# Sharing each loaded weight tile between two token halves in the expert stage of an eight-core recurrent-block and mixture-of-experts kernel

## What is computed

```
logits = xt @ gate_w.T;  scores = softmax(logits);  two experts are chosen per token -> cw[t, e]
h1 = einsum('td,efd->etf', xt, w1) + b1        # 8 experts, f = 2048, even and odd f are two halves
h3 = einsum('td,efd->etf', xt, w3) + b3
a  = swiglu(h1 * h3)                            # g = min(h[::2], 7), l = clip(h[1::2], -7, 7)
                                                # g * sigmoid(1.702 g) * (l + 1)
y  = einsum('etf,edf->etd', a, w2) + b2
out = sum_e cw[t, e] * y[e] + shared expert     # the shared expert has the same form
```

## Time and profile before

| | us |
|---|---|
| median of 7 runs | 5578.23 (5573.30 to 6060.81) |
| profiled execution, its own time | 5568.08 |
| its span on the slowest core (core 6) | 5566.5 |
| spans of the 8 cores | 5528.0 to 5566.5 |
| granted TensorE clock, mean, every core | 0.892 to 0.895 |
| TensorE matmul busy | 4030.7 (72%), 16176 recorded |
| TensorE weight load busy | 1617.7 (29%), 16496 |
| VectorE busy | 2357.5 (42%) |
| ScalarE busy | 1289.6 (23%) |
| POOL busy | 633.0 (11%) |

### The profile page before, as it was taken

One profiled execution on the slowest core, in us unless ns is written; L12 is line 12 of the kernel. 1 busy time (PEld: TensorE's weight loads), 2 busy tenths in 40 slices (PEclk: granted clock), 3 DMA queues, 4 the chain that ended last, 5 costly groups with the idle time before them and its releaser, 6 DMA issues.

```text
span 5566.5 us, 52221 instructions; the slowest of 8 cores (5528.0 to 5566.5 us)
## 1 busy us (share of the span) xinstructions
PE 4030.7 (72%) x16176; PEld 1617.7 (29%) x16496; DVE 2357.5 (42%) x3808; ACT 1289.6 (23%) x1875; POOL 633.0 (11%) x1187
## 2 busy tenths in 40 slices
PE   4565565664555666688889888887588888888885
PEld 1122121221211221233333333331233333333331
DVE  2433433323324233444554444544544554444544
ACT  1332332413224141111121111121111221111221
POOL 1011010111100111011111111110011111111110
PEclk8788788787887977899999999998799999999997
DMA  5354353435433442233334333332133343333341
GB/s 72 51 86 65 49 83 56 78 42 79 59 57 53 60 77 34 38 61 61 64 56 76 56 68 61 65 55 55 28 59 66 54 74 63 61 65 65 55 73 40
DMA packets 179709, 336.68 MB, mean 60 GB/s; under 512 B 19456, under 2 KB 39952, under 8 KB 179312
## 3 DMA queue, kind: packets, MB, share of 16 engines
q0 software_dynamic: 175280, 324.92, 36.1%
q1 hardware_dynamic: 4160, 8.39, 0.4%
HBM read 649.41 MB, written 8.39 MB: 118 GB/s over the span
## 4 chain that ended last, share of the span: by engine, by line
PE 64%; DVE 12%; ACT 11%; DMA 7%; issue 5%; DVEq 0%; POOL 0%; ACTq 0%; another core or an unknown queue 0%; POOLq 0%
PE pb L165 63%; ACT bufA L908 4%; DMA wi<-wi_xh 3%; DMA wi<-wi_gate 2%; DVE sa L532 1%; DVE sa L517 1%; ACT L513 1%; ACT ssf L513 1%; ACT sa L584 1%; DMA wo<-wout 1%; ACT L566 1%; DMA wg<-wgates 1%; DVE ssi L529 1%; DVE ssi L526 1%; ACT ssi L566 1%
## 5 line engine op out<-in xcount | busy, mean ns | idle before, releaser
L165 PE MATMUL pb<-xn,wq 128*128 128x512 bf16 x9030 | 2028.3, 379 | 275.8 <-ACT bufA L908 265.6
L165 PEld LDWEIGHTS pb<-xn,wq 128*128 128x128 bf16 x9216 | 882.1, 98 | 1427.8 <-issue 409.6
L165 PE MATMUL pb<-sxh,wg 128*128 128x512 bf16 x2256 | 592.5, 423 | 383.7 <-ACT ssf L566 361.2
L165 PE MATMUL pb<-a_s,w2s 128*128 128x512 bf16 x2258 | 544.5, 401 | 126.8 <-DVE a_s L963 124.5
L908 ACT ACTIVATE bufA<-pb,c_b1g 128x512 f32<-128x512 f32 x256 | 175.9, 687 | 1675.0 <-PE pb L165 1675.0
L165 PE MATMUL pb<-sxnbf,wi 128*128 128x512 bf16 x1128 | 315.1, 423 | 293.4 <-DMA wi<-wi_gate 127.5
L913 DVE SCALAR_TENSOR_TENSOR bufA<-pb,c_b3g,bufA 128x512 f32<-128x512 f32 x256 | 192.2, 751 | 672.7 <-ACT bufA L908 672.7
L165 PEld LDWEIGHTS pb<-sxh,wg 128*128 128x128 bf16 x2304 | 237.9, 106 | 738.0 <-issue 540.1
L165 PEld LDWEIGHTS pb<-a_s,w2s 128*128 128x128 bf16 x2304 | 231.7, 102 | 431.6 <-issue 195.0
L942 DVE TENSOR_TENSOR bufA<-bufA,bufC 128x512 f32<-128x512 f32 x288 | 199.5, 693 | 241.0 <-ACT bufC L937 241.0
L937 ACT ACTIVATE bufC<-bufA 128x512 f32<-128x512 f32 x288 | 181.3, 629 | 467.4 <-DVE bufA L932 467.4
(11 more groups left out here) (148 smaller groups left out, 3022.1 us busy)
## 6 DMA issues: line engine op xcount, KB each, us to landing
wg<-wgates POOLq DMA_DIRECT2D x192, 384.0 KB, 5.0
wq<-w1g POOLq DMA_DIRECT2D x128, 256.0 KB, 3.8
wq<-w3g POOLq DMA_DIRECT2D x128, 256.0 KB, 4.6
wq<-w1l POOLq DMA_DIRECT2D x128, 256.0 KB, 6.1
wq<-w3l POOLq DMA_DIRECT2D x128, 256.0 KB, 6.9
w2s<-w POOLq DMA_DIRECT2D x128, 256.0 KB, 4.1
wi<-wi_xh POOLq DMA_DIRECT2D x96, 256.0 KB, 3.9
wi<-wi_gate POOLq DMA_DIRECT2D x48, 256.0 KB, 4.5
```

What stands on the lines that cost most here:

```text
L165: t.matmul(o, l, r, start=s1, stop=s2),
```

## The change

The two token halves of a weight slice are run one behind the other, and the second of the two matmuls loads no weights.

- The four quadrants are split in two: a "G half" (quadrants 0 and 1) and an "L half" (2 and 3), 32 matmuls each. In each, k is the outer loop, and for each k four matmuls follow each other: first quadrant half 0, first quadrant half 1, second quadrant half 0, second quadrant half 1, into banks 0, 1, 2, 3. Both halves use the banks 0 to 3.
- After the G half come t1 of both halves on ScalarE, gg and g7 of both on VectorE, then sg and p1. After the L half come t2 of both, and ll, lc, p2, as of half 0 and then of half 1.
- Weight slots of quadrants 0 and 1 are released after the G half, those of 2 and 3 after the L half.
- In w2, k is the outer loop too: banks 4 and 5 in turn, 16 matmuls, then both `racc` additions.
- A new function after the build, `_mark_ldweights_reuse`, goes through TensorE's list and sets `ldweights=False` on each bf16 matmul whose weights are those of the matmul before it. This marks 4608 of the 9216 matmuls of the quadrants, 1152 of the 2304 of w2, 16 of the 32 b2 matmuls, and 120 of the 128 one-column matmuls of the first norm in the recurrent part.

The order of the other stages is the same. The diff, cut to its core:

```diff
+                            for k in range(NC_D):
+                                for j, (q_, t) in enumerate(
+                                        ((0, 0), (0, 1), (1, 0), (1, 1))):
+                                    b = 2 * q_ + t
+                                    t_mm(pb[b][:, :], wq[q_].slot(ql[q_])[:, k, :],
+                                         xn2[:, k, slice(t * ST, (t + 1) * ST)],
+                                         start=(k == 0), stop=(k == NC_D - 1),
+                                         waits=((bank_wait(b) if k == 0 else [])
...
+                            wq[0].done(ql[0])
+                            wq[1].done(ql[1])
+                            tcG = S.n["t"]
...
+                                a_op(lambda a, t=t, b_=bias(c_b1g, c_sb1g): a.activation(
+                                        out=bufA[:, t, :], in_=pb[t][:, :],
+                                        func=AF.Identity, bias=b_, scale=1.0),
+                                     waits=[("t", tcG)]
...
+                            bank_guard[0] = ("a", a1[0])
+                            bank_guard[1] = ("a", a1[1])
+                            bank_guard[2] = ("v", gg_v[0])
+                            bank_guard[3] = ("v", gg_v[1])
...
+                            for k in range(NC_D):
+                                for j, (q_, t) in enumerate(
+                                        ((2, 0), (2, 1), (3, 0), (3, 1))):
+                                    b = 2 * (q_ - 2) + t
...
+                            bank_guard[0] = ("a", a2[0])
+                            bank_guard[1] = ("a", a2[1])
+                            bank_guard[2] = ("v", ll_v[0])
+                            bank_guard[3] = ("v", ll_v[1])
...
-                                for k in range(E):
-                                    t_mm(pb[b][:, :], w2s.slot(li)[:, k, :],
-                                         a_s[:, k, tloc],
...
+                            for k in range(E):
+                                for t in range(2):
+                                    b = 4 + t
+                                    t_mm(pb[b][:, :], w2s.slot(li)[:, k, :],
+                                         a_s[:, k, slice(t * ST, (t + 1) * ST)],
...
+def _mark_ldweights_reuse(nc):
...
+                    key = (w.memref, w.offset, str(w.ap), str(w.dtype))
+                    both_bf16 = (w.dtype == mybir.dt.bfloat16
+                                 and ins.ins[0].dtype == mybir.dt.bfloat16)
+                    if key == last and both_bf16:
+                        new = dataclasses.replace(
+                            ins, name=nc.get_next_instruction_name(),
+                            ldweights=False)
```

More of the change, by code:

```diff
@@ new lines, in build_nc @@
+                            for t in range(2):
+                                v_op(lambda v, t=t, b_=bias(c_b3g, c_sb3g): v.scalar_tensor_tensor(
+                                        out=bufA[:, t, :], in0=pb[2 + t][:, :],
+                                        scalar=b_, in1=bufA[:, t, :],
+                                        op0=OP.add, op1=OP.mult),
+                                     waits=[("t", tcG), ("a", a1[t])],
+                                     tag=f"gg{p}{e}{m}{t}")
+                                gg_v[t] = S.n["v"]
+                                v_op(lambda v, t=t: v.tensor_scalar(
+                                        out=bufA[:, t, :], in0=bufA[:, t, :],
+                                        scalar1=7.0, scalar2=None, op0=OP.min),
+                                     tag=f"g7{p}{e}{m}{t}")
+                                g7_v[t] = S.n["v"]
@@ new lines, in build_nc @@
+                            for t in range(2):
+                                v_op(lambda v, t=t: v.tensor_tensor(
+                                        out=bufA[:, t, :], in0=bufA[:, t, :],
+                                        in1=bufC[:, t, :], op=OP.mult),
+                                     waits=[("a", sg_a[t])], tag=f"p1{p}{e}{m}{t}")
+                            for k in range(NC_D):
+                                for j, (q_, t) in enumerate(
+                                        ((2, 0), (2, 1), (3, 0), (3, 1))):
+                                    b = 2 * (q_ - 2) + t
+                                    t_mm(pb[b][:, :], wq[q_].slot(ql[q_])[:, k, :],
+                                         xn2[:, k, slice(t * ST, (t + 1) * ST)],
+                                         start=(k == 0), stop=(k == NC_D - 1),
+                                         waits=((bank_wait(b) if k == 0 else [])
+                                                + ([wq[q_].wait(ql[q_])]
+                                                   if (k == 0 and t == 0) else [])),
+                                         tag=f"ql{q_}{p}{e}{m}{t}")
@@ new lines, in build_nc @@
+                            wq[2].done(ql[2])
+                            wq[3].done(ql[3])
+                            tcL = S.n["t"]
+                            a2 = {}
+                            ll_v = {}
+                            for t in range(2):
+                                a_op(lambda a, t=t, b_=bias(c_b1l, c_sb1l): a.activation(
+                                        out=bufB[:, t, :], in_=pb[t][:, :],
+                                        func=AF.Identity, bias=b_, scale=1.0),
+                                     waits=[("t", tcL)], tag=f"t2{p}{e}{m}{t}")
+                                a2[t] = S.n["a"]
@@ L892, in build_nc @@
                             for t in range(2):
                                 tloc = slice(t * ST, (t + 1) * ST)
[L894 to L911, removed]
@@ L922, in build_nc @@
[L922 to L928, removed]
@@ L946, in build_nc @@
[L946 to L947 removed]
+                                v_op(lambda v, t=t, b_=bias(c_b3l, c_sb3l): v.scalar_tensor_tensor(
+                                        out=bufB[:, t, :], in0=pb[2 + t][:, :],
+                                        scalar=b_, in1=bufB[:, t, :],
+                                        op0=OP.add, op1=OP.mult),
+                                     waits=[("a", a2[t])], tag=f"ll{p}{e}{m}{t}")
@@ L961, in build_nc @@
                                          tag=f"p2{p}{e}{m}{t}")
[L962 to L968, removed]
+                                v_op(lambda v, t=t, m=m, tloc=tloc: v.tensor_tensor(
+                                        out=a_s[:, m, tloc], in0=bufA[:, t, :],
+                                        in1=bufB[:, t, :], op=OP.mult),
+                                     tag=f"as{p}{e}{m}{t}")
+                                as_prev[t] = ("v", S.n["v"])
+                            bank_guard[0] = ("a", a2[0])
+                            bank_guard[1] = ("a", a2[1])
+                            bank_guard[2] = ("v", ll_v[0])
+                            bank_guard[3] = ("v", ll_v[1])
                         as_done = ("v", S.n["v"])
@@ L977, in build_nc @@
                                 b = 4 + t
-                                for k in range(E):
-                                    t_mm(pb[b][:, :], w2s.slot(li)[:, k, :],
-                                         a_s[:, k, tloc],
[L981 to L991, removed]
+                                tc = stop_tc[t]
                                 if e == 0:
@@ L1085, in _ @@
                 S.replay("gpsimd", gpsimd, sems)
+    _mark_ldweights_reuse(nc)
     return nc
+def _mark_ldweights_reuse(nc):
+    import dataclasses
+    for f in nc.m.functions:
+        for bl in f.blocks:
+            il = bl.instructions
+            last = None
+            for i, ins in enumerate(il):
+                if isinstance(ins, mybir.InstMatmult):
+                    if ins.is_transpose:
+                        last = None
+                        continue
+                    w = ins.ins[1]
+                    key = (w.memref, w.offset, str(w.ap), str(w.dtype))
[5 more added lines that the diff above has]
+                            ldweights=False)
+                        il[i] = new
+                        nc.register_instruction(new)
+                    last = key
+                elif isinstance(ins, mybir.InstEventSemaphore):
+                    continue
+                else:
+                    last = None
 def _prep_shared(i):
```

80 lines of the change are left out of this document (49 added, 31 removed).

## The result

The changed kernel takes 6809.48 us (median of 12 runs, 6785.67 to 7080.03) and is 1.2219 times the kernel before (95% interval 1.2181 to 1.2257): some 1230 us slower than the median of before. The forecast was 6790.

A forecast was written before the change was run, and what follows sets the result against it. The expert stage was taken as bound by matmul column flow plus 0.98 us per handover. Losses of 220 + 392 + 181 + 418 = 1211 us on the profiled 5568 gave 6779, plus 10 for the median, rounded to 6790; range 6360 to 7010.

The forecast's parts named there:

- G to L handover: From G half to L half, bank 3's matmul waits for the second gg: 1.53 us lost, 144 times, 220 us.
- L to G handover: From L half to next G half, bank 3's matmul waits for the second ll: 3.11 us lost, 126 times, 392 us.
- w2: Between w2 output tiles, the next tile's second matmul waits for the second addition: 1.44 us lost, 126 times, 181 us.
- clock after G to L: TensorE's clock falls after the G to L stall: half of 1.69 us, 0.85, lost 144 times, 122 us.
- clock after L to G: TensorE's clock falls after the L to G stall: 2.35 us lost, 126 times, 296 us.
- weight loads: 5760 loads dropped from the two big loops lie under the matmuls: at most 14 us back, taken as nothing.
- signs named beforehand: Profile after: some 144 gg and 126 ll waits (over 2 us each), `racc` waits, some 5900 fewer loads, unchanged spacing, lower clock.
- Rival 1: In the m loop the stalls are as computed but the clock holds at 1.00: 6371 us, chance 0.14.
- Rival 2: The clock falls at every handover of the m loop: 7005 us, chance 0.12.
- Rival 3: Handovers are shorter because VectorE or ScalarE give the banks up sooner: about 6185 us, chance 0.05.
- Rival 4: Two matmuls with kept weights overlap, so the kernel is not slower: 5545 us, chance 0.03.
- note that p1 and the loads stay hidden: p1 fits under the L half and POOL's loads keep their order: costed at nothing.

The follow-up runs named there:

- e10: The changed kernel unaltered, run once more and profiled at 6781.68 us; 1.2189 times the kernel before.
- e4: The changed kernel with w2 in the old order (8 matmuls into bank 4, then 8 into bank 5); shortest 6602.01 us.
- e3: The changed kernel plus 1836 matmuls with unread results, put into idle bank 4 during the handover stalls; shortest 6375.08 us.
- e1: The changed kernel without the marks, so every matmul loads its weights again; 1.2229 times the kernel before, shortest 6797.67 us.
- e6: The kernel before with kept weights shared one quadrant at a time, 16 matmuls into two banks while two are read; 0.941 of the kernel before.
- e7: The kernel of e6 with every matmul loading its weights again; 0.9425 of the kernel before, shortest 5252.47 us.
- e5: The kernel before, same matmul order, but each bank read after its own 8 matmuls instead of all 32; shortest 5175.41 us.

## Why the prediction was right

Its terms, and what the runs and the trace of e10 gave. For the handovers I took the starts of all 9216 quadrant matmuls of that trace: the mean time from a half's last start to the fourth start of the next, less 0.38 for the last one's row and 1.63 for the same place before; for the clock, the time from the fourth to the 32nd start less 28 x 0.216. Before, the fourth start came 1.62 after the row's end by the same count.

| term | predicted, us | measured, us |
|---|---|---|
| G to L handover | 144 x 1.53 = 220 | 144 x (3.66 - 0.38 - 1.63) = 238 |
| L to G handover | 126 x 3.11 = 392 | 126 x (5.18 - 0.38 - 1.63) = 399 |
| w2 | 126 x 1.44 = 181 | 184 to 196 (e4) |
| these together | 793 | 813 (e3) |
| clock after G to L | 144 x 0.85 = 122 | 147, in 98 of 144 |
| clock after L to G | 126 x 2.35 = 296 | 243, in 126 of 126 |
| clock together | 418 | 423 (e3 against e1), 392 (m loops of e3 against e10) |
| weight loads | 0 | nothing beyond the intervals (e1, e6 and e7); at most 11 by stage (e1 against e10) |

The steps hold one by one. From before to e10 the m loops grow by 3328.0 - 2297.7 = 1030 us, 639 of them waits (e3) and 392 clock, and w2 by 733.3 - 549.3 = 184; together 1214, against 1211 predicted. The signs named beforehand are there: 144 and 126 waits, the latter of 311.6 / 126 = 2.5 us each, and 5896 loads fewer at an unchanged 0.216 us.

The handover lengths came from pitches between operations that the change did not alter, and were short by 0.06 to 0.12 us each. The weakest step was the clock, carried over from wout and from the wait for a_s: its split was off, 53 us too much after the long stall and 25 too little after the short one. After the short stall the prediction took half of a bound without a row for it; in fact a third of these handovers lost nothing and the others some 1.5 us each. That the total came within 3 us is luck: the waits were 30 us short and the clock 26 too long. Rival 1 (the clock holds) is refuted by the stretch at 0.50 in the trace after, and e3 shows that 6375, almost its 6371, is just what the kernel takes when the clock does hold. Rival 2 fails on the 46 G to L handovers without a loss. Rival 3 fails on the handovers, longer than computed. Rival 4 fails on the spacing, 0.216 in the changed kernel too, and on e1, e6 and e7. The note that p1 and the loads stay hidden holds too: no wait of TensorE on either appears.

The Trainium skill's page TensorE: Matmul & The Clock Gate describes, in "A second HAM failure mode: psum-queue depth-cycling", a clock that falls and returns between bursts when banks are cycled. The trace after agrees, 0.87 in the stretch from 5310 to 5350; but not every pause counts, since in e10 46 handovers from G to L and all those of w2 kept the clock. The 131 ns per 512-column matmul that the same page of the Trainium skill gives ("Back-to-back issue gap") are not borne out in any run: 0.216 us stands with and without kept weights.

## What to carry to other kernels

Read the start-to-start time of the matmuls before paying for fewer weight loads: at 0.216 us for 512 columns a load of 0.1 us is free. Interleaving several banks makes all of them end together and be wanted together, so the slowest reader of the set, with everything queued ahead of it on its engine, stands in front of TensorE; start each read on its own bank's last matmul, which gave 307 of the 395 us in e5; and if weights are to be shared, share them over two banks while two others are read (e6). A stall of some us costs once more through the clock, about half as much again here.

## What the runs showed of the hardware that was not expected

Matmuls whose result nobody reads made a kernel faster: 1836 more of them, 423 us less (e3). After the same stall of 3.3 us the clock was lost in 98 of 144 handovers, some 1.5 us each time, and kept in the other 46 (e10). In the trace of the changed kernel core 6 was granted 0.81 of the clock for 889 us, with 0.263 us from start to start; in that of e7, whose matmuls are denser, core 1 was for 2077 us, and in that of e5, as dense as e7, no core was. What sets it off no run here shows.
